# A two-pass graph kernel: early rows every fourth step, table split in steps of three, 17 quads from step 460

## The reference

```python
deg  = segment_sum(1, dst);  wsum = segment_sum(edge_weight, dst)
w    = edge_weight / maximum(wsum, EPS)[dst]
feat = relu(h @ W_pool + b_pool)
neigh = segment_max(feat[src] * w[:, None], dst)        # 0 where deg == 0
rst  = h @ W1_self + neigh @ W1_neigh + b1
h1   = relu(rst / maximum(norm(rst), EPS))
neigh2 = segment_sum(h1[src] * w[:, None], dst) / maximum(deg, 1)[:, None]
out  = x + relu(h1 @ W2_self + neigh2 @ W2_neigh + b2)
```

## Time and profile before

| | |
|---|---|
| median of 3 runs | 4011.11 us (4010.85 to 4014.95) |
| the profiled execution | 4012.82 us, its span 4011.1 us |
| busy share of the span | PE 83%, DVE 74%, ACT 34%, POOL 75% |
| gathers on POOL | 1415 in phase 0, 1463 in phase 1, 196 of node rows, 88 of early rows |
| phase 0 | from about 110 us to 1890 us |
| granted TensorE clock | half speed for most of the first 730 us, then full speed to the end of phase 0 |

### The profile page before, as it was taken

The page is one execution under the profiler, slowest core; times in us unless marked ns, Lnnn a source line. Parts: engine busy times, 40 slices in busy tenths (PEclk is TensorE's granted clock), DMA queues, the critical chain, the costliest instruction groups (busy, mean ns, idle before and its releaser), DMA issues. The chain is left out here.

```text
span 4011.1 us, 50027 instructions
## 1 busy us (share of the span) xinstructions
PE 3314.2 (83%) x15076; PEld 1706.3 (43%) x15331; DVE 2971.0 (74%) x6665; ACT 1349.1 (34%) x3970; POOL 2998.5 (75%) x3178
## 2 busy tenths in 40 slices
PE   4357763799999999994669999999999999999936
PEld 3245442344444444442423444444444444444424
DVE  6578876678888788775557778787877778787734
ACT  5345543333333333332553333333333333333310
POOL 7777777777777777776767777777777777777766
PEclk7566655899999999997579999999999999999965
DMA  6464333333333333333533333333343433333347
GB/s 202 128 184 142 120 116 129 109 112 116 112 112 119 109 111 120 108 109 115 148 108 115 114 119 127 121 124 122 115 130 114 128 117 119 127 119 117 121 130 196
DMA packets 271763, 501.67 MB, mean 125 GB/s; under 512 B 58900, under 2 KB 187412, under 8 KB 246660
## 3 DMA queue, kind: packets, MB, share of 16 engines
q1 hardware_dynamic: 170180, 290.72, 21.0%
q0 software_dynamic: 101312, 207.74, 18.3%
HBM read 260.23 MB, written 237.99 MB: 124 GB/s over the span
## 5 line engine op out<-in xcount | busy, mean ns | idle before, releaser
L559 POOL DMA_INDIRECT G<-h_tab,SRC x1463 | 1381.9, 945 | 457.5 <-issue 383.9
L559 POOL DMA_INDIRECT G<-feat_tab,SRC x1415 | 1341.9, 948 | 431.7 <-issue 365.3
L658 ACT ACTIVATE pM<-G,EW 128x128 f32<-128x128 f32 x1440 | 508.7, 367 | 1349.8 <-DMA G<-h_tab,SRC 596.5
L901 DVE TENSOR_SCALAR CP<-pH,kcode 128x1024 bf16<-128x1024 bf16 x1225 | 911.4, 744 | 2.5
L658 ACT ACTIVATE pT<-G,EW 128x128 f32<-128x128 f32 x1438 | 513.6, 367 | 969.6 <-DMA G<-h_tab,SRC 443.9
L901 DVE TENSOR_SCALAR U<-pR,kcode 128x1024 bf16<-128x1024 bf16 x735 | 547.1, 744 | 1.6
L1094 PE MATMUL pC<-CP,A 128*128 128x512 bf16 x1246 | 474.7, 381 | 36.5 <-DVE CP L901 34.7
L1095 PE MATMUL pC<-CP,A 128*128 128x512 bf16 x1248 | 475.4, 381 | 4.4 <-DVE CP L901 3.1
L1068 PE MATMUL pH<-CP 128*128 128x98 bf16 x1563 | 298.9, 359 | 198.7 <-DVE CP L856 198.6
L1094 PE MATMUL pM<-CP,A 128*128 128x512 bf16 x1150 | 438.1, 381 | 27.8 <-DVE CP L901 26.1
L840 DVE SCALAR_TENSOR_TENSOR S<-S,M,pM 128x128 f32<-128x128 f32 x780 | 270.4, 347 | 253.0 <-ACT pM L658 192.0
(11 more groups left out here) (184 smaller groups left out, 3971.7 us busy)
## 6 DMA issues: line engine op xcount, KB each, us to landing
scan<-S SPq DMA_DIRECT2D x97, 1032.0 KB, 4.3
scan<-S SPq DMA_DIRECT2D x97, 1024.0 KB, 4.2
G<-h_tab,SRC POOLq DMA_INDIRECT x1463
G<-feat_tab,SRC POOLq DMA_INDIRECT x1415
U<-own_tab SPq DMA_DIRECT2D x48, 256.0 KB, 4.2
CP<-codes SPq DMA_DIRECT2D x25, 256.0 KB, 5.5
feat_tab<-F SPq DMA_DIRECT2D x24, 256.0 KB, 2.4
own_tab<-A SPq DMA_DIRECT2D x24, 256.0 KB, 6.3
```

The costliest lines, as they stand in the source:

```text
L559: pool.indirect_dma_start(out=dst, out_offset=None, in_=table, in_offset=bass.IndirectOffsetOnAxis(ap=idx, axis=0)).then_inc(s, 16)
L658: act.activation(scaled(t), v, ACT.Copy, scale=EW[:, t:t + 1]).then_inc(s_mul, 1)
L901: dve.tensor_scalar(HOT[phase][:, k % NHOT, :], sources(phase).bitcast(BF16), kcode[:, j:j + 1], None, ALU.is_equal).then_inc(s_o2, 1)
```

## The change

- `XAT`: the 88 steps that use early rows are every fourth step from 128 (to 476) and not every fifth (to 563).
- Split of phase 0: a piece every 3 steps from step 164 (to 386) and not every 4 steps from step 160 (to 456).
- `Q1`: 17 quads of 63 steps from step 460 (to 1531), before 15 quads of 64 from step 568 (to 1528). 8 more steps of phase 0 have no gather, so 1407 gathers are left.
- Histogram: 2.5 batches a block (3 in even blocks, 2 in odd ones) in blocks 3 to 26, and 38 batches for blocks 27 to 91. DVE makes them at steps 3, 8 and 13 of the block, PE two steps later.
- Phase 1, the signals between engines and all buffers stay.

```diff
-XAT = {128 + 5 * i: i for i in range(K)}
+XAT = {128 + 4 * i: i for i in range(K)}
...
-SPL1 = 160
-Q1 = [(0, 568 + 64 * i, 64) for i in range(15)]
+SPL1 = 164
+Q1 = [(0, 460 + 63 * i, 63) for i in range(17)]
...
-SPLIT_STEPS = [{n: SPL1 + 4 * n for n in range(3 * NGR)}, {n: n * 2 // 3 for n in range(3 * NGR)}]
+SPLIT_STEPS = [{n: SPL1 + 3 * n for n in range(3 * NGR)}, {n: n * 2 // 3 for n in range(3 * NGR)}]
...
-HS = 34
+HS = 27
...
+def early_hists(b):
+    return max(0, min(b, HS) - H0) * 5 // 2
...
 def hist_of(b):
-    early = 2 * (HS - H0)
+    early = early_hists(HS)
     if b < HS:
-        return [k for k in (2 * (b - H0), 2 * (b - H0) + 1) if k >= 0]
+        return list(range(early_hists(b), early_hists(b + 1)))
     return [k for k in range(early, NB) if HS + (k - early) * (HE - HS) // (NB - early) == b]
...
+def hist_steps(b, lag):
+    return {(3, 8, 13)[i] + lag: k for i, k in enumerate(hist_of(b))}
...
-                for k in hist_of(b):
-                    if i == (3, 11)[k % 2]:
-                        one_hots(k)
+                if i in hist_steps(b, 0):
+                    one_hots(hist_steps(b, 0)[i])
...
-                    for k in hist_of(b):
-                        if t % T == (7, 15)[k % 2]:
-                            histogram(k)
+                    if t % T in hist_steps(b, 2):
+                        histogram(hist_steps(b, 2)[t % T])
```

## The result

The changed kernel takes 4049.07 us in the median of 4 runs (4046.33 to 4055.55), the kernel before 4010.98 us beside it. The ratio is 1.0097, with a 95% interval of 1.0085 to 1.011: 38 us slower. The forecast was 4037 us, 26 us slower, in a range of 4001 to 4052. The profiled execution took 4046.44 us, its span is 4044.7 us, 33.6 us over the span of before.

A forecast was written before the change was run, and what follows sets the result against it. POOL's gathers, 1.25 us each, were taken to bound the kernel. DVE falls behind 21 + 35 = 56 us, slots cover 20, POOL stands 36; less 10 saved, +26: 4037 us, range 4001 to 4052.

The forecast's parts named there:

- the cover: Slots of `G`: 13 lead slots, 16.25 us, plus DVE four steps further behind ACT, 3.75 us; together 20 us of delay hidden.
- 8 gathers, 10 us: Two more quads in phase 0 take away 8 gathers of 1.25 us each, saving 10.0 us at most.
- POOL never waits for a slot before, and the program's time is the count of gathers: Both phases before: the time is the number of gathers times 1.25 us, plus about 60 us at the seams.
- DVE's own work, 21 us behind: Blocks 10 to 22: DVE has 16.62 us of work a block against POOL's 15.0; steps 164 to 367 sum to 21 us.
- DVE's waits for PE, 35 us in about 20 places: At the split's copies, DVE waits for pieces behind batches on PE, 1 to 4.5 us each, 35 us in all.
- my list: DVE's waits for split pieces by step and block (11, 7, 1, 13, others), summing to 38.4 us at half clock.
- Behind by 56 us in all: Dense stretch of phase 0: 21 us of DVE's own work plus 35 us of waits put DVE 56 us behind.
- The place in time: POOL stands still for 36 us between about step 220 and step 380, all between 350 and 520 us.
- 1 and 2: Rivals: the saving comes through, 4001 to 4003 us, 14%; only part of the waits, 4003 to 4019 us, 13%.
- Rival 3: The 2.4 GHz clock holds all through the stretch: waits 25.6 us, standing 27 us, time 4028 us; 12%.
- Rival 4: PE and ACT fall behind too, each block costing 1 us more: 13 us more, 4050 us, up to 4060; 12%.
- The stretch of quads: 17 quads of 63 steps: PE at 95.5%, DVE at 84%, neither sets POOL's pace; no cost.

The follow-up runs named there:

- the third: Changed kernel with odd split pieces ahead of the batches on PE and two batches a block in blocks 10 to 23: 4001.99 us, ratio 0.9977.
- the fourth experiment: As the third, but with the quads of the kernel before (15 of 64 steps from step 568, 1415 gathers): 4010.74 us, ratio 1.0.
- sixth experiments: The kernel before with the early rows every fourth step alone: 4011.11 us, ratio 0.9999.
- experiment 1: Changed kernel with PE making the odd split piece right behind the even one, ahead of the batch: 4018.09 us, ratio 1.0019.

## Why the prediction was right, and where it was off

The direction, the steps and the mechanism came out as reckoned, and the time lay in the range. The size was 38 us in the medians and 33.6 in the profiled spans, for 26; one term of the sum, the cover, was nearly twice what the trace shows, and the small errors of two others cancel.

- *8 gathers, 10 us*: 8.75 us between the third and the fourth experiment. Right within about 1 us.
- *POOL never waits for a slot before, and the program's time is the count of gathers*: shown by the third and sixth experiments, which keep the pace at another load and come out by their count.
- *DVE's own work, 21 us behind*: not measured alone. With the waits nearly gone, POOL still stands 17 us (experiment 1); 17 and the cover of 11 less the 3.9 us of waits left are 24, which is an estimate.
- *DVE's waits for PE, 35 us in about 20 places*: 30.9 in 17 places, 1.8 us on average; 35.2 and 35.3 in the executions with 12 and 18 slots. Counted by DVE's combinations, they stand in the steps and blocks of my list: step 11 in blocks 12, 15, 18 and 21 has 11.9 us (12.0 reckoned), step 7 in blocks 10, 13, 16, 19 and 22 has 4.9 (7.0), step 1 in blocks 13 and 19 has 7.0 (8.4), step 13 in the same two has 4.1 (4.4), and all others 3.0 (6.6). Right.
- *Behind by 56 us in all*: block 10 ended at 328 us and block 23 at 579 us on ACT, so 13 blocks took 250.5 us where their 156 gathers would take 195: 55.5 us. I had blocks of 18 to 20 us from 13 to 23; they took 16.1 to 23.6 us, 19.6 on average.
- *The place in time*: I had POOL standing still from 350 to 520 us; its waits over the ordinary gap run from 383 to 574 us. The steps were right and the times not. Step 160 doesn't begin at about 330 us in the kernel before, as the text ahead of the prediction says, but at about 314 us on ACT; and 220 steps from there at 15 us a block, with 36 us of standing still, end at about 556 us, not at 520.
- *The slots cover 20 us*: **this is the term that failed.** In those 250.5 us POOL issued 165 gathers (the row below has 166, of which one lies on the border), 9 more than the 156 that were used up: the cover was 9 x 1.25 = 11 us, and 55.5 - 11 = 44 us is what POOL stood still. I had counted 13 free slots and a group of four steps (3.75 us) more. The trace shows 4 gathers ahead at the start of the stretch, not 3, and 13 or 14 at the ends of the blocks from 13 on, not 16 (at most 10 with 12 slots and 16 with 18, so each time two slots less than there are). That ACT reads slots in bursts of four and the refill follows the bursts would account for it; this wasn't tested. And the four steps that DVE may stand further behind ACT were no additional cover: at the end of block 10, and at that of block 13, DVE had combined 8 steps less than ACT had multiplied (in the kernel before 4 at that of block 10), so that room was in use when the stretch began. With 11 for 20 the sum is 21 + 35 - 11 - 10 = 35 us, where the spans have 33.6. The 24 for 21 of own work and the 31 for 35 of waits nearly cancel.
- *The rivals.* *1 and 2* (short waits): out. *Rival 3* (clock granted all through): out. The granted clock was 0.64, 0.66 and 0.60 in the three stretches, before 0.64, 0.63 and 0.60; PE was busy for 73, 68 and 75%, before for 70, 71 and 67%. In experiment 1, with PE at 78%, it was 0.65, 0.67 and 0.62. *Rival 4* (PE and ACT fall behind) had 4050 us, nearer to the measured 4049 than my 4037, but not for its reason: PE was not the bound, for it waited 78.8 us in 300 us for DVE's one-hots (the row below), and ACT waited 93.5 us for DVE at one bank. By the time alone one would have chosen the wrong mechanism.
- The stretch of quads, which I had at no cost, has none: POOL keeps its pace of 81 gathers in 100 us from 600 us to the end of phase 0. What 17 quads cost is the 1.7 to 1.9 us behind it (experiment 4), which no term of the sum had.

The wait of PE for the one-hots in the changed kernel, 300 to 600 us:

```profile
PE pH L1077 <- DVE CP L866: 78.8, 36, 3.9
```

The ends of the blocks 10 and 23 are the rows of ACT that fill the sums of the weights into `S` (L698 after), in the timeline of ACT:

```profile
328.36 0.21 ACT L698 ACTIVATE S<-WS 128x16 f32<-128x16 f32 x1
...
578.88 0.22 ACT L698 ACTIVATE S<-WS 128x16 f32<-128x16 f32 x1
```

Gathers of POOL from 328.4 to 578.9 us:

```profile
L569 POOL DMA_INDIRECT G<-feat_tab,SRC x166 | 156.5, 943 | 94.6 <-ACT pM L668 33.3 <-issue 32.0 <-ACT pT L668 29.3
```

What stays open: the median is 2.6 us over the profiled execution, and the four executions spread over 9 us, where those of before spread over 5. The waits at the split were 30.9 us in one execution and 35.2 and 35.3 in two others of nearly the same kernel; whether this is the chance of one execution or comes with the number of slots, no run separates.

## What to carry to other kernels

When one engine only keeps the count and everything else has to keep up, write down the work of each other engine per unit of that pace, stretch by stretch; an average busy share of 80% hides a block that needs 110%. Then go through the places where one in-order engine reads what another in-order engine makes, and look at what stands ahead of it in the maker's list: here one batch of unrelated work ahead of a piece cost more (31 us) than the work that DVE had too much (21 to 24 us), and moving the piece three steps up gave back 31 us in the medians with no work removed. Buffers pay for a deficit only once per stretch, with the number of slots between the usual lead and the lead at saturation (here 4 and 13 of 16), so take that number and not the count of slots.

## What was not expected of the hardware

A batch, 16 products of 98 columns with a weight load each, takes 3.03 to 3.09 us on PE at either level of the clock (3.07 us at a granted clock of 0.50 and 3.03 at 1.00 in the earlier trace rows; 3.08 after), although pieces of the split do follow it: the two bf16 pieces take 1.06 us in the one and 0.61 in the other. A first part in f32 is dearer than I had estimated, 1.93 us on PE in the row above at 367.36, and two of them in a row in experiment 1 (two records each) take

```profile
361.46 3.63 PE L1133 MATMUL pR<-A,ident 128*128 128x512 f32 x4
```

1.8 us a piece, 3.4 times a bf16 piece of 0.53 us. The four waits at step 11 show it: 3.6 us where the piece is a first part (blocks 12 and 21) and 2.3 us where it is not (blocks 15 and 18). A wait behind batch and group work, at step 1 of block 19, is as long (3.6 us) without a first part.
